# Causal attention: the maxima are split on GpSimd, and they are turned one step later

## Reference, cut to what matters

```python
q = (x @ wq).reshape(b, s, H, hd)          # 16 heads of 8 channels
k = (x @ wk).reshape(b, s, H, hd)
v = (x @ wv).reshape(b, s, H, hd)
scores = jnp.einsum('bqhd,bkhd->bhqk', q, k) / np.sqrt(hd)
scores = jnp.where(causal, scores, jnp.finfo(scores.dtype).min)
attn = jax.nn.softmax(scores, axis=-1)
o = jnp.einsum('bhqk,bkhd->bqhd', attn, v).reshape(b, s, d)
```

## Time and profile before

| | |
|---|---|
| median of 3 runs | 1192.98 us (1183.32 to 1194.06) |
| the profiled execution | 1189.37 us, its span 1187.6 us |
| busy over the span | PE 92%, DVE 68%, ACT 61%, POOL 29% |
| reduces of the causal stage (L1196, `da_`) | from 156.2 us on, 128 of them, 102.9 us |
| selects of the causal stage (L897) | 128 of 412 ns |
| mean granted clock of TensorE | 0.968 |

### The profile page before, as it was taken

The page is one execution under the profiler, slowest core; times in us unless marked ns, Lnnn a source line. Parts: engine busy times, 40 slices in busy tenths (PEclk is TensorE's granted clock), DMA queues, the critical chain, the costliest instruction groups (busy, mean ns, idle before and its releaser), DMA issues. The chain is left out here.

```text
span 1187.6 us, 35597 instructions
## 1 busy us (share of the span) xinstructions
PE 1097.9 (92%) x14750; PEld 562.0 (47%) x14750; DVE 810.4 (68%) x1312; ACT 729.9 (61%) x1464; POOL 340.4 (29%) x667
## 2 busy tenths in 40 slices
PE   6999899999899998889999999999988888899997
PEld 2344443333244443567767767766745333222222
DVE  4897478888533443377767767777716466999995
ACT  5313637888554434466675766666744373899994
POOL 0552203333235244333333224322113431100000
PEclk9999869999999999899999999999989997999999
DMA  5000054211093200601021021101100003511100
GB/s 203 1 0 1 8 153 150 57 45 31 4 183 76 71 1 0 125 14 10 8 20 10 8 17 10 11 8 9 11 6 1 1 14 83 202 44 44 44 17 36
DMA packets 134927, 51.61 MB, mean 43 GB/s; under 512 B 103968, under 2 KB 126512, under 8 KB 134256
## 3 DMA queue, kind: packets, MB, share of 16 engines
q1 hardware_dynamic: 134732, 49.32, 17.8%
q10 hardware_dynamic: 36, 0.02, 0.0%
HBM read 33.09 MB, written 15.81 MB: 41 GB/s over the span
## 5 line engine op out<-in xcount | busy, mean ns | idle before, releaser
L2489 DVE TENSOR_REDUCE re_nmax<-ps 128x1 f32<-128x512 f32 x256 | 159.0, 683 | 57.9 <-PE ps L2292 57.9
L2423 ACT ACTIVATE normed<-ps,re_nmax 128x512 f32<-128x512 f32 x256 | 154.9, 693 | 4.7 <-DVE re_nmax L2489 4.7
L2313 PE MATMUL ps<-const,normed 128*128 128x128 f32 x1024 | 147.0, 283 | 2.5 <-ACT normed L2423 2.2
L1100 ACT ACTIVATE ga_pt<-ps 128x512 f32<-128x512 f32 x256 | 139.2, 598 | 15.4 <-PE ps L983 13.8
L2429 ACT ACTIVATE re_pT<-ps 128x512 f32<-128x512 f32 x128 | 76.6, 599 | 116.2 <-PE ps L2313 116.0
L1196 DVE TENSOR_REDUCE ga_nmax<-ps 128x2 f32<-128x1024 f32 x128 | 146.7, 1216 | 1.4 <-PE ps L947 1.4
L2313 PEld LDWEIGHTS ps<-const,normed 128*128 128x128 f32 x1024 | 110.4, 142 | 28.7 <-issue 14.9
L1196 DVE TENSOR_REDUCE da_nmax<-ps 128x2 f32<-128x256 f32 (+3 forms) x128 | 102.9, 821 | 20.7 <-PE ps L958 18.8
L1100 ACT ACTIVATE da_pt<-ps 128x512 f32<-128x512 f32 (+3 forms) x256 | 96.7, 435 | 31.6 <-PE ps L983 28.9
L2509 DVE COPY re_pT<-ps 128x512 f32<-128x512 f32 x128 | 82.5, 685 | 34.1 <-PE ps L2313 34.1
L1659 DVE TENSOR_TENSOR ex_u<-ps,ex_s 128x512 f32<-128x512 f32 x48 | 32.8, 690 | 90.9 <-PE ps L1494 68.0
(11 more groups left out here) (398 smaller groups left out, 1983.9 us busy)
## 6 DMA issues: line engine op xcount, KB each, us to landing
ex_gates<-gates_scratch SPq DMA_DIRECT2D x4, 2048.0 KB, 15.9
da_qst<-da_stacks SPq DMA_DIRECT2D x32, 96.0 KB, 2.2
da_kst<-da_stacks SPq DMA_DIRECT2D x32, 96.0 KB, 2.3
ga_qst<-ga_stacks SPq DMA_DIRECT2D x32, 96.0 KB
ga_kst<-ga_stacks SPq DMA_DIRECT2D x32, 96.0 KB
da_stacks<-da_qkparts SPq DMA_DIRECT2D x6, 384.0 KB, 3.1
ga_stacks<-ga_qkparts SPq DMA_DIRECT2D x6, 384.0 KB, 2.7
weights<-in_weights SPq DMA_DIRECT2D x1, 2048.0 KB, 10.5
```

Source lines behind the costliest of these rows:

```text
L1100: nc.scalar.activation(pt[:, (4 * u + kt) % SLOTS, 2 * pr + par, q0:T], g.ps[:, st_bank(st_slot[t, par]), q0:T], ACT.Exp)\
L2313: last = nc.tensor.transpose(g.ps[:, bank_of("tile", s, idx), bass.ts(kt, 128)], p[:, QUAD_ORDER[idx], bass.ts(kt, 128)], g.c("ident"))
L2423: nc.scalar.activation(p[:, QUAD_ORDER[idx], :], g.ps[:, S_BANK + QUAD_ORDER[idx], :], ACT.Exp, bias=nmax[:, s % 2, idx:idx + 1]).then_inc ...
L2489: nc.vector.tensor_reduce(nmax[:, s % 2, idx:idx + 1], g.ps[:, S_BANK + quad, :], AX.X, ALU.max, negate=True).then_inc(maxed, 1)
```

## The change

Only for the causal stage:

- the four operations of `split_maxima` go from VectorE's queue to GpSimd's. There they stand at step 8(u + 1), ahead of the select that belongs to that step;
- the turn, its slot in the ring, and ScalarE's copy go from r1 to r2 (`TURN_AT`). In each engine's step they stand where they stood: on TensorE after the values, on ScalarE after the exponentials of the step;
- VectorE waits at r0 of unit u, from u = 2 on, until the split of unit u - 2 is done, as `nmax` has two buffers.

```diff
+    TURN_AT = 2 if causal else 1
...
-        if step % 8 == 1 and 8 < step < STEPS + 8:
+        if step % 8 == TURN_AT and 8 < step < STEPS + 8:
             turn_slot[step // 8 - 1] = len(st_ring)
...
+                    def split_maxima(u):
+                        pool.wait_ge(maxed, 8 * (u + 1))
+                        if u >= 2:
+                            pool.wait_ge(m_turned, u - 1)
+                        n = u % 2
+                        part = lambda k: mparts[:, n, :, :, k, :].rearrange("p q a r -> p a r q")
+                        nc.gpsimd.tensor_copy(part(0), nmax[:, n]).then_inc(split1, 1)
+                        pool.wait_ge(split1, u + 1)
+                        nc.gpsimd.tensor_tensor(mrest[:, n], nmax[:, n], part(0), ALU.subtract).then_inc(split2, 1)
+                        pool.wait_ge(split2, u + 1)
+                        nc.gpsimd.tensor_copy(part(1), mrest[:, n]).then_inc(split3, 1)
+                        pool.wait_ge(split3, u + 1)
+                        nc.gpsimd.tensor_tensor(part(2), mrest[:, n], part(1), ALU.subtract).then_inc(split4, 1)
...
+                    for step in range(STEPS + S_LAG):
+                        if causal and step % 8 == 0 and 8 <= step <= STEPS:
+                            split_maxima(step // 8 - 1)
+                        if causal and step >= S_LAG:
+                            select(step - S_LAG)
...
-                        if step % 8 == 1 and step // 8 - 1 in turn_slot:
+                        if step % 8 == TURN_AT and step // 8 - 1 in turn_slot:
                             turn_maxima(step // 8 - 1)
...
-                        if step % 8 == 1 and step // 8 - 1 in turn_slot:
+                        if step % 8 == TURN_AT and step // 8 - 1 in turn_slot:
                             copy_maxima(step // 8 - 1)
...
                         dve.wait_ge(scored, step + 1)
+                        if causal and r == 0 and u >= 2:
+                            dve.wait_ge(split4, u - 1)
...
-                        if r == 7:
+                        if not causal and r == 7:
                             split_maxima(u)
```

More of the change, by code:

```diff
@@ L889, in _, with select @@
                         front.gpsimd(pool)
[L890 to L898, removed]
+                    def split_maxima(u):
[11 more added lines that the diff above has]
+                        nc.gpsimd.tensor_tensor(part(2), mrest[:, n], part(1), ALU.subtract).then_inc(split4, 1)
+                    def select(t):
+                        u, r = divmod(t, 8)
+                        kt, pr = divmod(r, 2)
+                        q0 = first_query(kt)
+                        pool.wait_ge(exped, 2 * t + 2)
+                        square = pt[:, (4 * u + kt) % SLOTS, 2 * pr:2 * pr + 2, q0:q0 + 128]
+                        nc.gpsimd.affine_select(square, square, [[0, 2], [1, 128]], ALU.is_ge, 0.0, base=0,
+                                                channel_multiplier=-1).then_inc(selected, 1)
+                    for step in range(STEPS + S_LAG):
[3 more added lines that the diff above has]
+                            select(step - S_LAG)
                     if finish:
```

## The result

The changed kernel takes 1203.5 us (median of 4 runs, 1203.1 to 1207.0), the kernel before 1189.6 us (4 runs, 1183.3 to 1194.1): a ratio of 1.0134, interval 1.0091 to 1.0176. The forecast was 1203. The profiled execution took 1203.82 us with a span of 1201.8, against 1187.6 before: +14.2 us.

A forecast was written before the change was run, and what follows sets the result against it. The prediction took the cycle through the maxima's DMA landing before r6 as deciding: +0.83 us a steady round, +11.7 us over the units, from 1191.2 to 1203 us, range 1188 to 1213.

The forecast's parts named there:

- the landing decides: Path from the maxima's DMA issue to r6 is level with the reduce path, or at most 0.40 us short.
- The steady round: From r6 to issue 5.56, plus 1.03, plus landing 2.63: 9.22 us against 8.39, +0.83 a round.
- The quiet queue's 2.43: Lower bound for the landing of the maxima's DMAs, from the last load, in a quiet queue: 2.43 us.
- The sum: Delays of r6 over units 0 to 15 total +11.7 us; +9.3 with landing 2.43, +14.1 with 2.83.
- the starting point of 1191.2: Time before the change, taken halfway between the profiled execution and the median of the three runs shown: 1191.2 us.
- the cover: The split's parts on GpSimd stand 1.0 us before the turn wants them, 2.3 us in all before costing anything.
- VectorE's relief at 0: The split's 0.89 us a unit leaving VectorE only lengthens its idle time before r2: counted 0, bound -13 us.
- Idle time of VectorE before r2 above 1 us: Sign of being right, in a steady round of the changed profile; the idle time was 0.38 us before.
- The hidden landing: Rival: SyncE's DMA is ready in 1.8 us, so the 1.03 shift fits; 0 to +1 us, 1193; chance 0.14.
- VectorE as the limit: Rival: the path through VectorE's reduces is the bound, so the kernel gets faster, 1180 to 1189 us; chance 0.12.
- the late split: Rival: GpSimd's four operations exceed 2.3 us and the turn waits; with 0.7 each, 1211 us; chance 0.1.
- The fall of the clock: Rival: longer pauses return TensorE to half clock; a third of the stage there gives 1218 us; chance 0.07.

The follow-up runs named there:

- six copies more: Changed kernel with six more dependent copies, needed by nobody, on GpSimd ahead of each split: 1206.18 us, measured once.
- the first experiment: Changed kernel with the turn and its copy put back into r1, the split staying on GpSimd: 1190.26 us, ratio 1.0004 to the kernel before.
- the kernel with the issue at r4: Kernel before, with SyncE also waiting for r4's transposed scores before issuing the DMAs of the maxima: 1213.65 us, ratio 1.0218.
- both kernels with lag 15 and the turn in r1: Transposed scores 15 instead of 14 steps behind the scores, turn in r1: ratio 1.0101 with the split on VectorE, 1.0123 on GpSimd.
- all kernels of the table: Kernels before and changed and lag-14 variants, listed by issue after r6, landing and round; rounds 8.39 to 9.89 us.

## Why the prediction was right

**The cycle.** The step "the landing decides" held. Issue after r6: 5.56 + 1.03 = 6.59 forecast, 6.62 measured. The landing: 2.63 taken, 2.70 measured, between the bounds of 2.43 and 2.83. The steady round: 9.22 forecast, 9.32 measured. The estimate that the prediction drew from the Trainium skill (DMA: Bandwidth & Descriptors, Anatomy of one DMA), 2.7 to 2.8 us, was nearer than my middle, and the 2.70 agrees with it. That section gives its 2.0 us for DMAs issued through GpSimd, and SyncE issued these, so the prediction had carried the figure over. The quiet queue's 2.43 was no landing that anyone waited for on TensorE. That the first values wait for the copy of the output bank, and not for the select that the row before had named, is borne out: the row at 253.86 names ScalarE's copy behind the same 0.28 us.

**The sum.** By the start of r6, after against before:

| unit | forecast | measured |
|---|---|---|
| 0 | +0.8 | +0.21 |
| 1 | +0.7 | +1.44 |
| 2 and 3 | +0.5, +0.6 | +0.56, +0.37 |
| 4 to 14 | +9.1 | +9.89 |
| 15 | 0 | +0.02 |
| all | +11.7 | +12.49 |

Unit 15 is 316.87 against 304.38. A steady round is 0.93 us longer, 0.10 above the forecast: 0.07 from the landing and 0.03 from the issue. Unit 4, with 0.66, brings the mean down to 0.90.

In unit 0 the wait for the DMA grew from 0.42 us to 1.21, yet r6 came only 0.21 later. The stage's first scores stood at 155.45 us in this execution, 0.28 earlier than before (155.73). Counted from there r6 is 0.49 later and the turn 0.44: 12.83 us against 12.39. The forecast had +0.8, the whole block. But in the kernel before, the turn of unit 0 (168.12) stood right behind the end of its split (168.07), 0.51 us after the mask of its step had begun; in the changed kernel it stands 0.19 us after it. That waiting for the split is gone, and it takes 0.32 us off the move.

In unit 1 the granted clock was still 0.50 between 180 and 182 us; the kernel before had 1.00, in its busy time by stretch:

```profile
180.00:182.00 2.00, 2.00 (x48) 0.68 (x40) 1.77 (x2) 1.11 (x5) 0.86 (x3) 1.00 0.02 6
```

So more of this unit ran at the lower level than the 1.4 us that I had counted. It is luck that the errors of units 0 and 1 cancel (1.65 against 1.5).

**What passes on.** The last select ends the stage 13.6 us later (328.8 against 315.2), so 1.1 us came in behind the last r6. The granted clock over the last 12 us of the stage is 0.86. The same stretch of the kernel before, in its busy time by stretch:

```profile
304.00:316.00 12.00, 10.85 (x103) 3.10 (x100) 9.22 (x7) 7.50 (x20) 3.66 (x9) 1.00 0.01 1
```

There it was 1.00. That clock was not in the forecast. What brought it down is open, but the loss does not need it: the kernel with the turn alone has the same rounds and 1.00 in the same stretch (318 to 330 us), its last select stands 10.8 us behind the last r6 as in the kernel before, and its ratio is 1.0129. The stages behind moved by about 12 to 16 us at their various points and the span by 14.2, so the loss passed on whole, as the prediction said, with up to 2 us either way.

**The single time** was met by luck closer than the sum deserved: +11.7 was forecast and +13.9 came by the medians (+14.2 by the spans), and the starting point of 1191.2 was 1.6 us above the 1189.6 that four runs gave, so two errors of opposite sign nearly cancel.

**The split.** On GpSimd it took 1.23 us (1.3 forecast) and was ready 1.04 us before the turn (1.0 forecast); six copies more showed the cover to be 0.99. Counting VectorE's relief at 0 was right by the first experiment. The Trainium skill's rule that weighed against this edit (GPSIMD Engine Reference, 4.1 Engine selection: two-input operations about 2x slower on GpSimd) is not borne out in size at 128x16: the two subtractions take 0.230 and 0.268 us on GpSimd and 0.219 and 0.232 on VectorE, and the whole chain 1.23 us against 0.89, 1.4x. With the turn in r2 it cost nothing.

**A sign that was off.** "Idle time of VectorE before r2 above 1 us" showed 0.81. The freed time was spread, with 0.29 us before the reduce of r1 and 0.35 before r3. In the kernel with the split moved alone it was 1.09, so the sign belonged to the edit and not to the pair of them.

**The rivals.** The hidden landing fell by the 15 waits. VectorE as the limit fell by the first experiment, the late split by the cover. The fall of the clock did not happen in steady rounds: 1.00 from 184 to 310 us. But the same mechanism appeared in the kernel with the issue at r4 and in both kernels with lag 15 and the turn in r1, there behind pauses shorter than the 0.84 us of the changed kernel. That the changed kernel was spared is measured, not explained.

## What to carry to other kernels

When an engine waits for a tiny DMA, write the round as (work until the issue) + (landing) and look for the slack of the landing in a place where it is waited for; here the slack was 0.13 us, and each tenth of delay beyond it was paid in every round. A step moved by one place in one engine's order is paired with a lag somewhere else: try both together, since either alone can cost 1% and the pair nothing. Time freed on the busiest-looking vector engine is worth nothing while its instructions behind the freed place wait for someone else's result.

## What the runs showed of the hardware

- Two DMAs of a few rows in one queue land 2.69 to 2.70 us after the first issue, in the steady rounds of all kernels of the table where TensorE waits for them; the issue came up to 1.6 us later than before, and the landing did not change by more than 0.01. Single rounds differ: 3.04 us once with the issue at r4, and 2.73 and 2.98 in the kernel before, beside other traffic. SyncE issues each in about 0.73 us (1.47 for two, 0.72 for one).
- A DMA issued by ScalarE right behind its own copy cost ScalarE 0.80 us of idle time before its next activation, as much as it saved.
- On GpSimd casts and subtractions of 128x16 take 0.23 to 0.27 us (0.20 to 0.28 on VectorE), and six dependent copies 1.49 us together, some 0.25 each.
- TensorE kept its full clock (1.00, the level of 2.4 GHz) through a pause of 0.84 us in every round of the changed kernel. It fell to about half for some 3.5 us in 4 rounds of the kernel with the issue at r4, whose pauses are some 1.3 us, and not behind the pause of 1.65 us there. With lag 15 and the turn in r1 it fell in one round (split on VectorE) and in three (split on GpSimd; mean 0.96 from 184 to 310 us), with pauses of 0.59 us before the values and up to 0.55 us before the turn. So here no length of a single pause separates the rounds that lost the clock from those that kept it.
